# Early-fusion block on one core: unused bf16 matmuls on TensorE ahead of the first stacks and among the maxima of the first chunk

## The reference

```python
h = _L0_tok_ref(x, L0_tok_W)                 # patches -> rfft -> @ W.T: (8, 1024, 64)
h = jnp.concatenate([h, txt], axis=1)        # + 32 text tokens: L = 1056
h = h + _L0_attn_ref(_layernorm(h, axis=-1), L0_attn_w_qkv, L0_attn_w_proj, L0_attn_b_proj)
h = h + _L0_ffn_ref(_layernorm(h, axis=-1), ...)

# attention, 4 heads of 16
attn = jnp.einsum('bhnd,bhmd->bhnm', q, k) * SCALE
attn = jax.nn.softmax(attn, axis=-1)
out = jnp.einsum('bhnm,bhmd->bhnd', attn, v)
...
# experts: 8 of them, the two best of each token weighted by their softmax
h = jax.nn.gelu(xf @ w1 + bb1, approximate=False)
y = h @ w2 + bb2
return (acc + we[:, None] * y, None)
```

## Time and profile before

| | us |
|---|---|
| median of 3 runs | 999.66 |
| lowest, highest | 997.33, 1000.4 |
| profiled execution | 1001.97 |
| its span, first to last instruction | 1000.2 |
| TensorE busy | 899.0 (90%) |
| VectorE busy | 573.0 (57%) |
| ScalarE busy | 494.4 (49%) |
| mean granted TensorE clock | 0.922 |

### The profile page before, as it was taken

One profiled execution on the slowest core, in us unless ns is written; L12 is line 12 of the kernel. 1 busy time (PEld: TensorE's weight loads), 2 busy tenths in 40 slices (PEclk: granted clock), 3 DMA queues, 4 the chain that ended last, 5 costly groups with the idle time before them and its releaser, 6 DMA issues. The chain is left out here.

```text
span 1000.2 us, 17890 instructions
## 1 busy us (share of the span) xinstructions
PE 899.0 (90%) x5900; PEld 374.9 (37%) x5900; DVE 573.0 (57%) x1201; ACT 494.4 (49%) x1189; POOL 138.7 (14%) x148
## 2 busy tenths in 40 slices
PE   5665899999999989999999999999965989899996
PEld 5241322433342343343243334333412535354443
DVE  4025565578874557876557887788230553636331
ACT  0020254466664536665446676666533454555552
POOL 0010100011010011101001101001000344444443
PEclk9965589899999988999989999999876999999998
DMA  8329351027551005536002305100006655382731
GB/s 153 57 47 163 62 62 31 3 35 119 97 69 44 2 4 67 117 67 110 2 1 30 40 2 68 44 3 1 1 5 141 120 126 117 80 184 52 155 78 22
DMA packets 55864, 64.58 MB, mean 65 GB/s; under 512 B 23893, under 2 KB 41825, under 8 KB 55777
## 3 DMA queue, kind: packets, MB, share of 16 engines
q1 hardware_dynamic: 55777, 63.46, 35.5%
HBM read 36.73 MB, written 2.43 MB: 39 GB/s over the span
## 5 line engine op out<-in xcount | busy, mean ns | idle before, releaser
L887 DVE TENSOR_REDUCE max_parts<-bank 128x1 f32<-128x512 f32 x512 | 329.6, 685 | 137.4 <-PE bank L1075 134.5
L811 ACT ACTIVATE probs<-bank 128x384 f32<-128x384 f32 (+1 forms) x768 | 313.4, 466 | 191.1 <-PE bank L1038 189.6
L1038 PE MATMUL bank<-q_stack,k_stack 99*128 99x384 bf16 (+1 forms) x768 | 229.9, 329 | 4.9 <-ACT probs L811 4.2
L1075 PE MATMUL bank<-k_stack,q_stack 96*128 96x512 bf16 x512 | 208.4, 409 | 17.2 <-DMA k_stack<-part 13.2
L1016 PE MATMUL bank<-probs,v_tiles 128*32 128x384 f32 (+1 forms) x1536 | 160.2, 490 | 5.4 <-ACT heads_out L796 5.0
L1038 PEld LDWEIGHTS bank<-q_stack,k_stack 99*128 99x128 bf16 x768 | 72.2, 99 | 196.1 <-ACT probs L811 146.1
L1285 ACT ACTIVATE hid<-bank,biases 128x352 f32<-128x352 f32 x192 | 96.0, 552 | 84.8 <-PE bank L1329 84.7
L1304 DVE SCALAR_TENSOR_TENSOR prod<-bank,biases,cwb 128x352 f32<-128x352 f32 x96 | 55.8, 582 | 120.1 <-PE bank L1317 103.0
L1329 PE MATMUL bank<-x,w 128*128 128x352 bf16 (+1 forms) x576 | 105.2, 320 | 6.3 <-DMA x<-part 6.3
L1317 PE MATMUL bank<-hid,w_sb 128*64 128x352 f32 x384 | 79.2, 491 | 7.7 <-DVE prod L1304 4.0
L1052 PE MATMUL bank<-x,tok_m 128*64 128x512 f32 x256 | 68.5, 634 | 9.4 <-DMA text_in<-in_txt 8.0
(11 more groups left out here) (146 smaller groups left out, 704.2 us busy)
## 6 DMA issues: line engine op xcount, KB each, us to landing
cwb<-gates_by_expert SPq DMA_DIRECT2D x16, 1056.0 KB, 12.1
x<-in_x SPq DMA_DIRECT2D x64, 256.0 KB, 6.9
q_stack<-part SPq DMA_DIRECT2D x48, 132.0 KB, 6.1
k_stack<-part SPq DMA_DIRECT2D x48, 132.0 KB, 6.6
x<-part SPq DMA_DIRECT2D x32, 132.0 KB, 2.5
h_res<-h_new SPq DMA_DIRECT2D x4, 528.0 KB, 3.0
h_all<-h_res SPq DMA_DIRECT2D x4, 528.0 KB, 3.1
h<-h_all SPq DMA_DIRECT2D x8, 264.0 KB, 3.2
```

Of the source, the lines that this page charges most:

```text
L811: nc.scalar.activation(probs[:, group % 3, h, 0:n], src, ACT.Exp, scale=SCALE).then_inc(exp_done, 1)
L887: nc.vector.tensor_reduce(max_parts[:, c, H * j + h, i % 2:i % 2 + 1], src[:, :], AX.X, ALU.max)\
L1038: last = nc.tensor.matmul(bank[:, 0:n], ks[par][0:ROWS + 3, h, P * kt:P * kt + P], qs[par][0:ROWS + 3, h, QC[qc]], start=True, stop=True)
L1075: last = nc.tensor.matmul(bank[:, :], queries(h, j), ks[par][0:ROWS, h, HALF * (i % 2):HALF * (i % 2) + HALF], start=True, stop=True)
```

## The change

A maximum step of sample 0 that belongs to the first chunk (`c == 0`, par 0) is preceded by matmuls whose result nobody reads: 36 ahead of the first step, one ahead of each of the 24 others. Each is 128 rows of `part0` by 128 of its columns, against 512 columns, in bf16, and writes `o_bank`. The 36 wait for part 0 to be complete and stand ahead of the wait for the stacks. No other instruction is moved, on any engine.

```diff
 PV_LAG = 2 * H
+BUSY_STACK = 36
...
+                def keep_busy(n):
+
+                    for _ in range(n):
+                        nc.tensor.matmul(o_bank[:, :], qk_part[0][:, 0:P], qk_part[0][:, 0:HALF], start=True, stop=True)
+
                 def side(stage, i, t, par, pair, g):
                     rows = None if par is None else slice(D * par, D * par + D)
+                    in_first = stage == "maxima" and par == 0 and isinstance(t, int) and t == 0
+                    if in_first and i[0:2] == (0, 0):
+                        pe.wait_ge(part1_done, NCH)
+                        keep_busy(BUSY_STACK)
+                    elif in_first and i[0] == 0:
+                        keep_busy(1)
                     if stage == "maxima":
```

## The result

| | before | changed |
|---|---|---|
| median, us | 1000.21 (15 runs) | 1004.21 (15 runs) |
| lowest, highest | 995.59, 1004.75 | 1002.39, 1007.86 |
| ratio, 95% interval | | 1.0046 [1.0027, 1.0064] |
| profiled execution, its span | 1001.97, 1000.2 | 1003.1, 1001.2 |
| mean granted clock | 0.922 | 0.939 |

The account below looks back on a forecast made before the run. VectorE and transfers bound the front, TensorE at half clock only 107.95 to 131.47 us. Clock lost in the gap +1.2, kept -0.2, middle +0.5 on median 999.66 gives 1000.2 us; range 990 to 1003.5.

Parts of the forecast that it names:

- Every sign that it had named for the front of the kernel: Full clock from 76 to 78 us, unused matmuls over by 82 to 83.5, first maximum at 85.5 to 86, half clock from 108.
- The added work in the wait: 36 unused matmuls from 72.5 us, while TensorE waits for the stacks: over by 82.3 to 83.3, before 85.7, costing nothing.
- the coin: Whether the 2.4 to 3.4 us idle before the first maximum drop the clock to half: even odds, +1.2 or -0.2 us.
- The singles: 24 unused matmuls beside first-chunk maxima: hidden at full clock; at half, 0.25 us per step, 1.0 to 1.8 us lost.
- The clock at 107.95: Lean TensorE work after about 99.8 us returns the clock to half before slot 0's attention stream, which runs as before.
- The step on which the sum was said to turn: Whether raised clock survives from 99.8 us to the stream at 107.95: expected lost, so no gain there.
- The rival: Clock holds until the stream at 107.95 to 131.47, saving 11.5 us there, about 990 us in all; chance 0.15.
- The slower rival: Clock does not rise under the unused matmuls in the stack wait: +8.3 us, 1008 us; chance 0.08.
- The slower side: Whole kernel measurably slower, beyond about 0.3% or 3 us: chance 0.10.
- The rise within the stream: Full clock at 131.47 us as before; an earlier rise after 12 us of stream would win 5 to 6 us, chance 0.07.

## Why the prediction was wrong

It gave 1000.2 us, 990 to 1003.5, and 0.66 for no measurable difference. Measured were 1004.21, slower by more than its interval. Every sign that it had named for the front of the kernel came as said; its steps:

- **The added work in the wait: right.** 9.8 to 10.8 us predicted, 10.21 measured; the rise after 4.6 us, between the 3.9 and 5.7 taken; idle 3.07 us of the 2.4 to 3.4 left; and the coin fell on the side of a lost clock, at 87.45.
- **The singles: right, and their price a little too high.** 0.7 us were lost up to the first exponential of slot 0, against +1.2 in that case. The rise came 5.0 us into the dense stretch that began at 85.87, within the 3.9 to 5.7 taken. But the fall came only at 87.45, so the half clock lasted 3.4 us and some four steps were slow, not 4 to 7; the first score did take 0.39 us.
- **The clock at 107.95: right.** It fell at 104.52, and the stream began at 0.50. The step on which the sum was said to turn held. The rival was priced at 11.5 us in the stream and 10 in all: filling the gap gave 10.0 at 141, part of which was the draw, and 8.4 in all by the ratio once the input came earlier.
- **The slower rival did not happen.** The slower side came by something else, of which the prediction had no term.
- **The rise within the stream: not foreseen as this large.** The forecast said that the stream would run as it does now, and that a rise a little sooner would move a run by itself. In the profiled execution it came 10 us sooner, which won 4 us in slot 0. Kernels without the unused work had it too.
- **The step that failed: the change costs nothing outside the stretch that it stands in.** "No other instruction is moved" is true of the order and false of the addresses. 120 instructions ahead of the loop shift its start within the pieces of 16384 bytes, an estimated 256 instructions each, in which instructions arrive as I read the traces. The earlier trace rows held the wait of 2.75 us ended by "issue" at 371.91, and the prediction used it only as a gap that cost the clock; it never asked what "issue" was there. The term was missing, not mis-sized: 3.4 us at that jump, by the traces, and 3.7 to 5.5 us by the ratios, between kernels of one kind with 120 and with 160 or 256.
- **The own range was also too narrow on that side.** The three kernels with a second wait lie 4.6 to 6.5 us above before, of which the traces explain 3.2 to 3.4 at the jump. At the start of the experts, where VectorE waits for the gates' transfer, the changed kernel lost 3.0 us against before (its half-clock stretch there lasted 6.82 us, that of before 3.41), but kernels with a single wait lost as much there (3.7, the changed one with 160) or won 1.9 (with 256), so it is not tied to the change. Whether the remaining 1 to 3 us are this, or a further cost of the place, is open.

## What to carry to other kernels

The 120 instructions added here ahead of a loop cost 3.2 to 3.4 us around the loop's jump back, and 0.7 us where the unused work stands: look in the trace for a wait ended by "issue" in the middle of a series, and try the same change with a few dozen instructions more before judging it. Unused matmuls were worth their place here only where the clock that they raised lasted until the stretch that TensorE bounds, and where the next thing that this stretch waits for was brought forward with it; either half alone measured as nothing (1.0011) or a quarter (0.9977) of what both gave (0.9916). The place of the rise in one profiled execution was a draw here, near 121 us or near 130: compare it in several kernels before calling it an effect.

## What the runs showed that I had not expected

- The gap behind the jump that I read as a wait for instructions: 2.58 to 3.03 us in every kernel, and a second of 1.81 to 2.10 us with 120 instructions added and none with 160, 176 or 256.
- Behind idle time of 3.07 and 3.00 us ahead of the first maximum (the changed kernel, twice) the clock fell from 1.00 to 0.50, and behind 2.12 (46 in the wait, later loads), and it did not behind 2.18 and 2.33 (the changed kernel with 256 and with 160): the coin that the prediction tossed there fell on either side.
- The stream of slot 0 gets its full clock near 121 us or near 130, with the same kernel or nearly: 121.40 and 120.51 without any unused work, 121.59 and 122.10 with it, 131.47, 130.74 and 129.63 without, 130.05 and 128.79 again with it.
- Single matmuls beside VectorE-bound steps raised the clock 6.0 us after the first step, where the steps alone, with TensorE nominally busy 13.72 of 14.1 us, left it at 0.50.
